# Moving weight folds, warming products and an early delta in a three-layer kernel on one core

## Time and profile before

| | |
|---|---|
| median of three runs | 2204.65 us |
| profiled execution | 2206.03 us |
| its span, first to last instruction | 2204.3 us |
| mean granted TensorE clock | 0.896 of full |
| busy: PE / DVE / ACT / POOL | 74% / 82% / 68% / 70% |
| chain that ended last | DVE 37%, issue 20%, PE 18%, POOL 12%, ACT 10% |
| largest lines of the chain | DVE scan L1321 12%, POOL gathers L1429 10%, DVE dots L1244 7% |

### The profile page before, as it was taken

How to read it: one execution, slowest core, us unless ns; L and a number is a source line. 1 busy time by engine, 2 the same in 40 slices (tenths; PEclk the granted TensorE clock), 3 DMA queues, 4 the chain that set the end, 5 groups by cost and what they waited for, 6 DMA issues and landing times.

```text
span 2204.3 us, 24242 instructions
## 1 busy us (share of the span) xinstructions
PE 1638.3 (74%) x6099; PEld 908.3 (41%) x6186; DVE 1805.9 (82%) x4265; ACT 1496.9 (68%) x3199; POOL 1538.0 (70%) x1147
## 2 busy tenths in 40 slices
PE   5677586878787978787887878787878777856533
PEld 2233243434444544344544445444445444434322
DVE  1989697889998989999899989899999999743221
ACT  3555575857786867878677868777777776546532
POOL 1023636288888888888888888888888888767344
PEclk8899898989999989999999999999999998967766
DMA  2001111022323222232222232222323222333212
GB/s 53 10 0 34 53 30 57 24 70 72 89 67 89 70 81 74 72 84 71 84 67 84 72 87 68 82 71 72 86 69 85 67 82 73 97 93 108 58 53 81
DMA packets 79898, 151.03 MB, mean 69 GB/s; under 512 B 20584, under 2 KB 46592, under 8 KB 79680
## 3 DMA queue, kind: packets, MB, share of 16 engines
q0 software_dynamic: 49152, 134.28, 21.3%
q1 hardware_dynamic: 29344, 14.65, 2.4%
q10 hardware_dynamic: 1248, 0.34, 0.1%
HBM read 145.01 MB, written 4.19 MB: 68 GB/s over the span
## 4 chain that ended last, share of the span: by engine, by line
DVE 37%; issue 20%; PE 18%; POOL 12%; ACT 10%; another core or an unknown queue 1%; DMA 1%; DVEq 1%; ACTq 0%; POOLq 0%
DVE hp L1321 12%; POOL rows L1429 10%; DVE rows L1244 7%; PE bank L709 5%; DVE hp L1330 4%; DVE hp L1311 4%; ACT rows L984 3%; PE bank L668 3%; PE ysum L768 3%; DVE top L1211 2%; ACT flip L965 1%; DVE st L1182 1%; DVE mask L1218 1%; ACT L914 1%
## 5 line engine op out<-in xcount | busy, mean ns | idle before, releaser
L1429 POOL DMA_INDIRECT rows<-in_experts,index x1024 | 1302.7, 1272 | 360.7 <-issue 297.8
L1321 DVE TENSOR_TENSOR_SCAN hp<-dA,hp 128x1024 f32<-128x1024 f32 x256 | 617.9, 2414 | 10.5 <-ACT dA L1005 8.5
L768 PE MATMUL ysum<-hp,ident 128*128 128x512 f32 x1024 | 504.1, 619 | 18.5 <-POOL hp L1444 16.4
L1005 ACT ACTIVATE dA<-delta,decay 128x511 f32<-128x511 f32 x512 | 334.1, 710 | 46.8 <-POOL delta L1459 19.3
L1244 DVE CUSTOM_DVE_ANT_0 rows<-rows,xn 128x128 f32<-128x128 f32 x1024 | 272.2, 328 | 97.1 <-DMA rows<-in_experts,index 97.0
L984 ACT ACTIVATE rows<-rows,coef 128x128 f32<-128x128 f32 x1024 | 308.8, 390 | 39.4 <-DVE coef L1251 39.4
L1311 DVE TENSOR_TENSOR hp<-du,bcast 128x1024 f32<-128x1024 f32 x256 | 307.1, 1199 | 22.6 <-POOL du L1463 15.6
L751 PE MATMUL bcast<-split,pick 128*128 128x512 bf16 x438 | 154.1, 397 | 188.1 <-DVE hp L1311 175.9
L768 PEld LDWEIGHTS ysum<-hp,ident 128*128 128x128 f32 x1024 | 201.5, 198 | 185.0 <-issue 139.8
L1444 POOL TENSOR_TENSOR hp<-hp,c_row 128x1024 f32<-128x1024 f32 x48 | 115.3, 2403 | 231.0 <-ACT c_row L1022 230.6
L709 PE MATMUL bank<-rows,ident 128*128 128x256 f32 x1024 | 248.6, 399 | 35.4 <-ACT rows L984 35.4
(11 more groups left out here) (179 smaller groups left out, 2190.2 us busy)
## 6 DMA issues: line engine op xcount, KB each, us to landing
rows<-in_experts,index POOLq DMA_INDIRECT x1024, 2.8
x_in<-in_x SPq DMA_DIRECT2D x16, 256.0 KB, 3.9
x_res<-in_x SPq DMA_DIRECT2D x16, 256.0 KB, 4.4
y<-x SPq DMA_DIRECT2D x16, 256.0 KB, 2.7
rows<-in_taps SPq DMA_DIRECT2D x1, 512.0 KB
rows<-in_wq_t SPq DMA_DIRECT2D x1, 512.0 KB, 5.5
rows<-in_in_proj_t ACTq DMA_DIRECT2D x1, 256.0 KB
rows<-in_key_t SPq DMA_DIRECT2D x1, 128.0 KB, 5.5
```

What stands on the lines that cost most here:

```text
L768: mm = nc.tensor.matmul(ysum[:, j, :], ident[:], hp[:, BUFFER[k], j, :], start=(k == 0), stop=(k == NS - 1))
L1005: op = nc.scalar.activation(dA[:, n % NDA, j, 1:T], delta[q][:, j, 1:T], ACT.Exp, scale=decay[:, j, n:n + 1])
L1321: nc.vector.tensor_tensor_scan(flat, dA[:, n % NDA, :, :].rearrange("p a b -> p (a b)"), flat, 0.0, ALU.mult, ALU.add).then_inc(scanned, 1)
L1429: pool.indirect_dma_start(e.rows[:, t, h, :], None, A["experts"], bass.IndirectOffsetOnAxis(ap=e.index[:, t, h:h + 1], axis=0)).then_inc(e ...
```

## The change

Four edits. TensorE executes 24 products of `ident16` by the zeroed `split[0]` into `bcast[0]` at slot 0 of iteration -1, once `cleared` is 2. `fold_weights` becomes two functions: `fold_keys` (through L723) at slot 34 of iteration -1, after `pe_conv` and ahead of `pe_xproj` in the code, and `fold_biases` at slot 36, after `pe_xproj` and ahead of `pe_rest`. `pool_delta` stands at slot 55 instead of 63 in iterations with i < 2, that is for batches 0, 1 and 2. Vector's and Scalar's programs are unchanged.

```diff
--- before.py
+++ after.py
@@ -50,6 +50,8 @@
 OFFSET = {PRE: 1, CORE: 0, POST: -1}
 DEPTH = 4
 LAST_ITERATION = NB - 1 + DEPTH
+FOLD_SLOTS = (34, 36)
+WARM = 24
 LOOP_FROM, LOOP_TO = 5, 15
 
 TURN = 4 * NS
@@ -215,6 +217,11 @@
     "pool_fetch_e2": (POST, (203, 209, 219, 227)),
 }
 
+EARLY_TO = 2
+EARLY_SLOTS = {
+    "pool_delta": (PRE, (55,)),
+}
+
 
 POOL_STATES = (1, 9, 11)
 DVE_STATES = tuple(n for n in range(NS) if n not in POOL_STATES)
@@ -228,6 +235,8 @@
 def due(stage, i, q, slot):
 
     phase, slots = SLOTS[stage]
+    if isinstance(i, int) and i < EARLY_TO and stage in EARLY_SLOTS:
+        slots = EARLY_SLOTS[stage][1]
     last = isinstance(i, int) and i >= NB and stage in LAST_SLOTS
     for k, own in enumerate(slots):
         new = LAST_SLOTS[stage][1][k] if last else own
@@ -713,7 +722,7 @@
                     half_done.remove(k)
                     fill(k, i, m, stage, half, e.added, 2, 1)
 
-            def fold_weights():
+            def fold_keys():
 
                 pe.wait_ge(weights_in, 16 * LOADS)
                 for g in range(GR):
@@ -723,11 +732,19 @@
                 nc.tensor.matmul(ysum[0:NS, 0, NS:NS + 1], b_mat[:], b_wb[:], start=True, stop=True,
                                  skip_group_check=True).then_inc(folded, 1)
 
+            def fold_biases():
+
                 nc.tensor.matmul(ysum[:, 1, 0:1], w_ff1[:], b_ff2[:], start=True, stop=True, skip_group_check=True)
                 nc.tensor.matmul(ysum[:, 1, 1:2], w_d[:], b_y[:], start=True, stop=True, skip_group_check=True)
                 pe.wait_ge(cleared, 3)
                 nc.tensor.matmul(ysum[:, 1, 2:3], w_gate[:], b_y[:], start=True, stop=True,
                                  skip_group_check=True).then_inc(folded, 1)
+
+            def warm(count):
+
+                pe.wait_ge(cleared, 2)
+                for k in range(count):
+                    nc.tensor.matmul(bcast[0][:, 0, :], ident16[:], split[0][:], start=True, stop=True)
 
             def iteration(i, q, has):
                 for k in busy:
@@ -753,6 +770,8 @@
 
                 for slot in range(TURN):
                     n, part = divmod(slot, TURN // NS)
+                    if isinstance(i, int) and i == -1 and slot == 0:
+                        warm(WARM)
                     if PRE in has and slot == TURN - 4:
                         spread(b[PRE], split[1 - q], 0)
                     if CORE in has and part == 0:
@@ -798,6 +817,8 @@
                                                   xrT[:, NK - 1:NK - 1 + T], start=True, stop=True)
                         mm.then_inc(conv_mm, 1)
                         fill(0, i, m, "pe_conv", k, conv_sb, 2 * NH, k)
+                    if isinstance(i, int) and i == -1 and slot == FOLD_SLOTS[0]:
+                        fold_keys()
                     for m, r, _ in due("pe_xproj", i, q, slot):
                         claim(0, i)
                         pe.wait_ge(silu_done, at(m, 1))
@@ -826,8 +847,8 @@
                     if PRE in has and slot == TURN - 1:
                         for k in range(1, NBC):
                             spread(b[PRE], split[1 - q], k)
-                    if isinstance(i, int) and i == -1 and slot == TURN - 1:
-                        fold_weights()
+                    if isinstance(i, int) and i == -1 and slot == FOLD_SLOTS[1]:
+                        fold_biases()
 
                     for m, r, _ in due("pe_out", i, q, slot):
                         claim(1, i)
```

## The result

The changed kernel took 2210.26 us (median of 20 runs, 2206.96 to 2215.22), the kernel before in the same session 2205.57 (20 runs, 2200.71 to 2211.87): ratio 1.0021, 95% interval 1.0014 to 1.0028. It is slower by about 4.7 us (3.1 to 6.2) where +2.7 was forecast. That is 0.21%, at the edge of the 0.2% that the measurement tells from no change, which lies inside the interval. The profiled execution took 2212.60 us, with a span of 2210.6.

What follows compares the result with a forecast made beforehand. Bound at the start by folds holding back iteration 0, and at the passage from iteration 1 to 2 by Pool's gathers in series with Vector. Start -3.3 plus early delta +6.0 gives +2.7: 2207.3 us, range 2201.5 to 2212.0.

Steps and rivals of the forecast that it cites:

- Delta ahead of the gathers: Iteration 1 on Pool: early delta waits for Scalar's log with 32 gathers queued behind it; gathers end later, +6.0 us.
- Convolution: Start, TensorE: warming keeps the clock at 2.4 GHz, so batch 0's first eight convolution products run faster, -1.5 us.
- the first rival: Clock drops again before the convolution and the gathers keep their full delay of 7.4: +6.9 us, 2211.6; chance 0.19.
- Key folds: Iteration -1, TensorE: key folds fill the gap before xproj and delay it slightly, +0.6 us, at worst +1.6.
- Bias folds: Iteration -1, TensorE: bias folds behind xproj run mostly while Scalar copies its result out, +0.1 us, at most +0.4.
- The feed no longer behind Vector's preparation: End of iteration -1: Vector's first feed waits for du alone and the first scan comes sooner, -2.0 us.
- Start together: Up to batch 0's first scan: warming, both folds and the earlier feed sum to -3.3 us, carried through iteration 0.
- the main case: Start's gain plus the early delta's cost in iteration 1: +2.7 us, own range +0.5 to +4.8; chance 0.55.
- The forecast's own distance: Iteration 0's first scan to batch 2's scan 3, 205.0 us before; growth under 4 us or shrinkage would show it wrong.
- The third rival: No change: clock stays at 2.4 GHz through xproj and the two dt products, -0.6 us, 2204.0; chance 0.12.
- The second: Faster: the gathers' delay is slack, -3.3 us, or up to 8.8 more; chance 0.14 together with the fourth rival.
- The fourth: Early delta does nothing because iteration 1 is not moved: -3.3 us; chance 0.14 together with the second rival.

Runs made afterwards that it cites:

- no_early2: Changed kernel without the early delta, warming and both folds kept, timed again on another chip: 2201.29 us, ratio 0.9985 to the kernel before.
- pool_wait: Kernel before, delta late as it was, but Pool's first fetch of batch 0 waits for Scalar's log of batch 2: 2212.02 us, ratio 1.0032.
- slot57: Changed kernel with the early delta at slot 57 instead of 55, behind the first eight gathers, on the slow chip: 2270.77 us, ratio 0.9999 to the kernel before.
- slot57b: Changed kernel with the early delta at slot 57 instead of 55, timed again on another chip: 2202.57 us, ratio 0.9981 to the kernel before.
- early_only: Kernel before with the early delta at slot 55 alone, no warming or moved folds, on the slow chip: 2282.93 us, ratio 1.0041 to the kernel before.
- early_only2: Kernel before with the early delta at slot 55 alone, timed again on another chip: 2210.52 us, ratio 1.0025 to the kernel before.
- warm_only: Kernel before with the 24 warming products alone, folds at slot 63: 2204.17 us, ratio 0.9993 to the kernel before.
- folds_only: Kernel before with key folds at slot 34 and bias folds at slot 36 alone: 2205.02 us, ratio 1.0002 to the kernel before.
- no_early: Changed kernel without the early delta, warming and both folds kept, on the slow chip: 2269.44 us, ratio 0.9996 to the kernel before.
- bridge: No early delta, 31 warming products and three more between transposes and batch 0's convolution, on the slow chip: 2272.01 us, ratio 0.9996 to the kernel before.

## Why the prediction was right, and where its sizes were off

- *Delta ahead of the gathers, +6.0.* Measured +5.95 in the profiles, +5.5 us in time alone (and 8.0, with a wide interval, as the distance of the changed kernel from no_early2). That it fits to 0.05 is luck: the three profiles with the early delta at slot 55 gave 63.0 to 63.3, those with no early delta and no added wait 57.0 to 57.6. The mechanism is not: the steps held one by one: idle time 7.22 (7.4), delta lengthened by the scan, gathers from 16.2 us behind state 11's product (16.0), five lengthened gathers, Vector's wait for du replaced by a wait for the dot of tile 0. pool_wait and slot57 show the cause and not only the size: the wait without the move costs 6.35, the move without the wait 0 to 0.6 (slot57, slot57b).
- *Transposes, -0.5.* Measured -0.46.
- *Convolution, -1.5.* This is the failed term: +0.1 in the changed kernel's profile. The forecast took a pause of 0.78 us as the nearer case. The pause was 1.66, and after it came 0.66 us of work and another pause of 0.78. What I had put into the first rival, that the clock drops again, happened in four of the six profiles with 24 products. The reading behind the term was weak too: I took 5.24 us, from one profile, as what the convolution costs without warming, and the five profiles without it have 5.12 to 6.55, 5.95 in the mean. So the warming may gain in the mean even where the clock falls.
- *Key folds, +0.6.* +0.34 for the start of xproj against silu's end. Beyond the forecast xproj itself was 0.44 longer, all of it at 1.2 GHz, while before its end ran faster, and each of the two subtracting products took 0.61 instead of 0.39, together another 0.44. These 0.9 us are why du is late although the start is ahead. In the other profiles xproj took 3.3 to 3.8 with and without the moved folds. The subtracting products took 0.61 in five of the nine profiles with moved folds and in one of the five without, so whether the folds have a part in it is open. The upper bound of +1.6 for the folds was too low: it priced a key product at 1.2 GHz from five of them, and where all 32 ran at a granted clock of 0.50 they took 7.03 us, 3.2 more than the 3.80 here.
- *Bias folds, +0.1.* The folds end at 37.71 and Scalar's copy, which the first subtracting product also needs, at 37.77, so they held nothing up: 0. (The product's own row is missing from the trace.)
- *The feed no longer behind Vector's preparation, -2.0.* -1.77 against the profile before (5.48 to 3.71), -3.5 against early_only and early_only2.
- *Start together, -3.3.* -1.2 by the first scan in this profile, of which 0.3 is an earlier first transpose that no term explains. In time it is -3.3 by no_early2 (0.9985, interval -1.3 to -5.1 us), but -0.8 as the changed kernel's +4.7 less early_only2's +5.5, and -1.1 as the sum of warm_only and folds_only. A gain is shown, its size is not.
- *The sum.* +2.7 forecast, +4.7 measured with an interval of 3.1 to 6.2. The parts alone are +5.5, -1.5 and +0.4 and add to +4.4. With nothing for the convolution the prediction's own terms give +4.2, so this one term accounts for most of the 2.0 that were missing; the result is the main case's early delta with the first rival's clock. The forecast's own distance (205.0 from the first scan to scan 3 of batch 2) grew to 209.3, by 4.3; that is 5.95 less the 1.6 that iterations 0 and 1 took less up to Pool's product of state 11. The forecast named less than 4 as the sign of being wrong, and the scatter of iteration 0 alone, 2 us, could have given that: a poor test, passed with luck.
- The third rival, a clock that stays up through xproj and the dt products, is not seen: the second pair of dt products took 2.07 or 2.08 in each of the fourteen profiles. The second, slack behind the gathers, is refuted by pool_wait. The fourth, that the delta does not move, by the profile.

## What to carry to other kernels

Before moving an operation forward in an engine's list, look at when its input is ready and at what is then queued behind it: a wait of 7 us ahead of 32 gathers costs nearly all of its length, however idle the engines that wait for the moved result. Where two idle times in one passage end on different things, the later one decides; removing the first turned into the second here. Place the moved step behind the work that fills its wait (slot 57 for 55), though here that only removed the loss and won nothing measurable over not moving it. Before taking a time from one profile as what a step costs, compare it across profiles of kernels that share the step, and judge edits of 1 or 2 us by many executions, since one profile of this kernel scatters by more.

## What the runs showed of the hardware

The clock of TensorE in the start went with the pause behind the warming. Where the warming ended 0.79 and 0.85 us ahead of the transposes, the first eight convolution products took 3.67 us, as fast as the next eight; where it ended 1.39 to 1.93 ahead, they took 5.15 to 5.37, and in the changed kernel's profile the granted clock fell from 1.00 to 0.50, from 2.4 to 1.2 GHz, just as the convolution began. A full TensorE does not by itself keep the clock up: in the kernel before it fell to 0.50 at 49.6, in the midst of the key products that had run without a pause since 46.43.

In these rows a Vector instruction with two SBUF operands and a Pool product took turns, and each side was lengthened by the other: 0.17 us became 2.35 for 16 elements, a scan of 2.28 became 5.12, a Pool product of 2.35 became 4.06 to 4.24. Which of two goes first cannot be read from the starts of their rows: that scan's row begins at 212.34, 0.62 us before the row of the delta that ended ahead of its work. The Trainium skill (SBUF — State Buffer, section "SBUF: two separate sides") says that Vector with two SBUF inputs and a GpSimd instruction that reads SBUF take one port pair in turns, each for its whole instruction. These rows agree.

One chip ran the kernel before 68 us slower (2274) than the others. Against the profile of the same kernel from another chip, Pool's last product, near 1870 us, is 11 to 14 us later in no_early, slot57 and bridge and 23 in early_only; the other 44 to 52 us are lost behind it, in the drain. In no_early Scalar stands for 28.10 us (5.78 in no_early2) ahead of an instruction whose last visible input was ready at 1925.2, 20.5 us before it:

```profile
1945.73 0.69 ACT L1063 ACTIVATE outT<-bank,b_ff 128x512 f32<-128x512 f32 x1 [28.10 <-remote]
```

TensorE stands with it for 21.35 us, while Pool goes on issuing gathers. What they waited for is in no row, and was not tried.
